# Turning the router product around in a fused conv-gate and mixture-of-experts block: router columns held, tokens streamed

## The reference, cut to what matters

```python
x = x + conv_gate(layernorm_over_channels(x))      # per sample and channel: a gate from mean, max, std and a median
t = tokens(x)                                      # 2048 tokens of 512 channels
h = layernorm(t)
logits = h @ router_w.T                            # 8 experts
top_vals, top_idx = top_k(logits, 1)
out = sigmoid(top_vals) * glu(h, expert top_idx)   # 8 experts of 512 x 512
out = out + glu(h, shared)
x = t + out
```

## Time and profile before

| what | us |
|---|---|
| median of 3 runs | 444.68 (442.83 to 445.02) |
| the profiled execution, its own time | 442.36 |
| the profiled execution, its span | 440.4 |
| TensorE matmuls busy | 402.2 |
| TensorE weight loads busy | 317.8 |
| VectorE busy | 235.2 |
| ScalarE busy | 192.8 |
| GpSimd busy | 191.8 |

### The profile page before, as it was taken

The page is one execution under the profiler, slowest core; times in us unless marked ns, Lnnn a source line. Parts: engine busy times, 40 slices in busy tenths (PEclk is TensorE's granted clock), DMA queues, the critical chain, the costliest instruction groups (busy, mean ns, idle before and its releaser), DMA issues.

```text
span 440.4 us, 7684 instructions
## 1 busy us (share of the span) xinstructions
PE 402.2 (91%) x2051; PEld 317.8 (72%) x2052; DVE 235.2 (53%) x525; ACT 192.8 (44%) x319; POOL 191.8 (44%) x262
## 2 busy tenths in 40 slices
PE   7867599899999989999999799999999999999981
PEld 3424388687878878888887687887878888777860
DVE  6879534786345442333687157456275736474330
ACT  4986257755762534542103245153264324361120
POOL 4896631555233543587021972425324340614110
PEclk9989999999999998999999899999999999999996
DMA  8900101011111551114344367626556764723100
GB/s 297 374 2 0 48 25 48 1 48 50 48 49 48 170 237 49 48 48 144 121 140 125 153 231 285 216 82 250 217 192 221 245 203 140 249 89 121 44 33 18
DMA packets 15886, 56.24 MB, mean 128 GB/s; under 512 B 2607, under 2 KB 2607, under 8 KB 12400
## 3 DMA queue, kind: packets, MB, share of 16 engines
q1 hardware_dynamic: 10976, 40.93, 25.7%
q0 software_dynamic: 4880, 14.95, 10.1%
HBM read 43.28 MB, written 13.63 MB: 129 GB/s over the span
## 4 chain that ended last, share of the span: by engine, by line
PE 75%; ACT 6%; DVE 6%; issue 5%; POOL 5%; DMA 1%; DVEq 0%; SPq 0%; POOLq 0%; ACTq 0%
PE GU L1531 42%; PE YHX L1531 22%; PE YHX L1523 3%; PE YHX L1516 3%; PE YHX L1560 2%; ACT w_raw L706 2%; ACT a_tiles L654 1%; POOL roots L434 1%; ACT hT L753 1%; ACT scratch L672 1%; PE A L1417 1%; DMA x_sb<-x_tok 1%; ACT scratch L676 1%; POOL w_parts L460 1%; POOL tok_rstd L427 1%
## 5 line engine op out<-in xcount | busy, mean ns | idle before, releaser
L1531 PE MATMUL GU<-w_parts,xT 128*128 (+1 forms) x864 | 218.4, 402 | 5.1 <-issue 4.3
L1531 PEld LDWEIGHTS GU<-w_parts,xT 128*128 128x128 f32 x864 | 159.9, 191 | 41.4 <-issue 9.9
L1531 PE MATMUL YHX<-w_parts,hT 128*128 (+1 forms) x432 | 108.2, 399 | 2.2 <-DVE hT L1099 2.2
L1531 PEld LDWEIGHTS YHX<-w_parts,hT 128*128 128x128 f32 x432 | 78.6, 188 | 19.1 <-issue 3.6
L577 POOL DMA_INDIRECT out<-x_sb,scatidx x20 | 28.8, 1438 | 105.9 <-DVE x_sb L1364 96.9
L753 ACT ACTIVATE hT<-YHX 128x512 fp32r<-128x512 f32 x36 | 21.5, 598 | 109.7 <-PE YHX L1523 109.7
L1099 DVE TENSOR_TENSOR hT<-YHX,hT 128x512 fp32r<-128x512 f32 x36 | 24.8, 690 | 71.1 <-ACT hT L753 70.9
L1105 DVE TENSOR_TENSOR hidden<-hidden,GU 128x512 f32<-128x512 f32 x36 | 24.7, 686 | 52.0 <-issue 42.7
L743 ACT ACTIVATE xT<-YHX 128x512 fp32r<-128x512 f32 x37 | 22.1, 598 | 61.8 <-PE YHX L1516 61.5
L1359 DVE TENSOR_TENSOR w_parts<-w_raw,w_parts 128x2048 f32 x19 | 43.5, 2289 | 5.0 <-ACT w_parts L852 3.2
L852 ACT ACTIVATE w_parts<-w_raw 128x2048 f32 (+1 forms) x21 | 39.4, 1912 | 0.0
(11 more groups left out here) (233 smaller groups left out, 448.8 us busy)
## 6 DMA issues: line engine op xcount, KB each, us to landing
w_raw<-weights SPq DMA_DIRECT2D x27, 1024.0 KB, 5.4
xn_d<-tiles SPq DMA_DIRECT2D x16, 256.0 KB, 2.0
z_d<-x_sb SPq DMA_DIRECT2D x16, 256.0 KB, 2.3
x_sb<-x_tok SPq DMA_DIRECT2D x7, 512.0 KB, 7.2
x_sb<-x_tok SPq DMA_DIRECT2D x2, 256.0 KB, 2.9
tiles<-xn_d,tokidx POOLq DMA_INDIRECT x21, 4.5
x_sb<-z_d,tokidx POOLq DMA_INDIRECT x20, 3.6
out<-x_sb,scatidx POOLq DMA_INDIRECT x20
```

The costliest lines, as they stand in the source:

```text
L1531: last = pe.matmul(dst, left[:, lp, kc, :], wset(q, k, wp, kc), start=(i == 0), stop=(i == 3 * KC - 1))
```

## The change

`router_parts` becomes [128, 4, 128]: 16 columns of the router as before and 112 columns of zeros, which GpSimd sets at the start (one more constant, `N_CONSTS` 18). For tiles 0 to 14 `route(t)` loads the router's 128 columns of a chunk as the stationary side and streams the two parts of the turned tile through, 256 columns in one matmul, four matmuls in all. The bank then holds, in its first 16 partitions, the logits' rows, once for each part of the tile. VectorE adds the two into `logit_rows` (16 by 128). TensorE turns these rows back (one transpose of 16 partitions, 16 columns out) at the head of `route(t + 1)`, and VectorE copies them into `logit_parts` in `keep_logits(t + 1)`. Tile 15 is routed in the old way. `logit_parts` and `logit_rows` lie in `scratch`.

```diff
-        router_parts = sb("router_parts", [P, KC, 2, E], F32R)
+        router_parts = sb("router_parts", [P, KC, P], F32R)
...
+        logit_rows = scratch[0:2 * E, 2 * C:2 * C + P]
+        logit_parts = scratch[:, 2 * C + P:2 * C + P + NT * 2 * E].rearrange("p (t e) -> p t e", e=2 * E)
...
+            pool.memset(router_parts[:, :, 2 * E:P].bitcast(F32), 0.0).then_inc(consts, 1)
...
             def keep_logits(t):
                 dve.wait_ge(logits, t + 1)
-                dve.tensor_copy(logit_parts[:, t, :], th[:, 0:2 * E]).then_inc(logits_used, 1)
+                if t:
+                    dve.tensor_copy(logit_parts[:, t - 1, :], th[:, 2 * P:2 * P + 2 * E]).then_inc(logits_used, 1)
+                if t < NT - 1:
+                    dve.tensor_reduce(logit_rows[:, :], th[0:2 * E, 0:2 * P].rearrange("p (h t) -> p t h", h=2), AX_X, ALU.add).then_inc(rows_kept, 1)
+                else:
+                    dve.tensor_copy(logit_parts[:, t, :], th[:, 0:2 * E]).then_inc(logits_used, 1)
...
                 pe.wait_ge(xlo, t + 1)
                 if t:
-                    pe.wait_ge(logits_used, t)
+                    logits_read(t - 1)
+                    pe.transpose(th[:, 2 * P:2 * P + 2 * E], logit_rows[:, :], ident[0:2 * E, 0:2 * E])
                 for kc in range(KC):
+                    if t < NT - 1:
+                        last = pe.matmul(th[:, 0:2 * P], router_parts[:, kc, :], xT[:, x_slot(t), :, kc, :],
+                                         start=(kc == 0), stop=(kc == KC - 1))
+                        continue
                     for lp in (HI, LO):
-                        last = pe.matmul(th[:, 0:2 * E], xT[:, x_slot(t), lp, kc, :], router_parts[:, kc, :, :].rearrange("p h e -> p (h e)"),
+                        last = pe.matmul(th[:, 0:2 * E], xT[:, x_slot(t), lp, kc, :], router_parts[:, kc, 0:2 * E],
                                          start=(kc == 0 and lp == HI), stop=(kc == KC - 1 and lp == LO))
                 last.then_inc(logits, 1)
+
+            def logits_read(t):
+
+                if t < NT - 1:
+                    pe.wait_ge(rows_kept, t + 1)
+                pe.wait_ge(logits_used, t if t < NT - 1 else NT)
```

More of the change, by code:

```diff
@@ L48 @@
 }
-N_CONSTS = 17
+N_CONSTS = 18
 FIRST_CONSTS = 13
@@ L156, in program @@
         warm = sb("warm", [P, 2])
-        logit_parts = sb("logit_parts", [P, NT, 2 * E])
         route_w = sb("route_w", [P, NT])
@@ L256, in program @@
         logits_used = sem("logits_used")
+        rows_kept = sem("rows_kept")
         chosen_ready = sem("chosen_ready")
@@ L1146, in _ @@
             dve.wait_ge(router_in, 16)
-            own(dve.tensor_copy(router_parts[:, :, HI, :], router_w[:, :, :]))
-            dve.tensor_tensor(router_parts[:, :, LO, :], router_w[:, :, :], router_parts[:, :, HI, :].bitcast(F32), ALU.subtract).then_inc(router_ready, 1)
+            own(dve.tensor_copy(router_parts[:, :, 0:E], router_w[:, :, :]))
+            dve.tensor_tensor(router_parts[:, :, E:2 * E], router_w[:, :, :], router_parts[:, :, 0:E].bitcast(F32), ALU.subtract).then_inc(router_ready, 1)
             measure_x1(2)
@@ L1637, in _ @@
                 visit(n, BEGIN)
-                pe.wait_ge(logits_used, max(t for m in range(n) for t in TURNED_AT.get(m, ())) + 1 if n else 2)
+                logits_read(max(t for m in range(n) for t in TURNED_AT.get(m, ())) if n else 1)
                 transpose_h(n, n % 2)
@@ L1677, in _ @@
             gate_product(n + 1, x_slot(n + 1), 0, 0)
-            pe.wait_ge(logits_used, NT - 1)
+            logits_read(NT - 2)
             transpose_h(n, 0)
@@ L1684, in _ @@
             gate_product(n + 2, x_slot(n + 2), 0, 0)
-            pe.wait_ge(logits_used, NT)
+            logits_read(NT - 1)
             transpose_h(n + 1, 1)
```

## The result

The changed kernel takes **440.23 us** (median of 7, 439.7 to 442.95) against 444.47 us before (7 runs): a ratio of 0.9924 with a 95% interval of 0.9895 to 0.9953. The forecast was 441.8 in a range of 439.2 to 445.2, with 0.57 on faster by over 0.5%. Sign, range and size came out right. The reasons did so only in part, as the two traces show.

A forecast was written before the change was run, and what follows sets the result against it. The prediction took TensorE, busy 402.2 of 440.4 us, as the bound. Nine middle tiles gave -3.0 us, tile 0 -0.14, tile 11 +0.14, tile 15 +0.11: -2.9 on 444.68, so 441.8 us, range 439.2 to 445.2.

The forecast's parts named there:

- What bounds the kernel: TensorE, 75% of the chain: shorter routes pay for twelve of sixteen tiles; at tiles 3, 4, 6, 7 TensorE only waits longer.
- Eight pairs become four of 256 columns: In each route of tiles 0 to 14, a load and matmul pair stays at 0.1125 us with 256 columns streamed.
- rival C: In each route, load and stream don't overlap at 256 columns: 0.22 us a pair, +1.8 us, 446.5; chance 0.08.
- The 98 ns a pair that the prediction set aside: Skill page's estimate for 256 columns: a middle route 0.06 us cheaper, the sum nearly 1 us better; not used.
- One transpose more: Turning the logits' rows back on TensorE costs a whole pair, 0.11 us; middle route minus 0.34 us, tile 15 plus 0.11.
- VectorE: New reduction of 256 elements at the end of `keep_logits`: 0.42 us a tile, hidden in a normal iteration.
- two places: Ahead of routes 1 and 11 TensorE waits for the reduction: 0.31 us more behind route 0, 0.48 behind route 10.
- The memset: GpSimd's zeros at the start, 448 elements a partition: at most 0.84 us, ahead of idle time, costing nothing.
- The sum: All tiles on the chain together: -2.9 us, from 444.68 to 441.8 us.
- Rival A: Behind routes 10 and 11 the clock's fall, costing 1.54 us, goes too: 440.2 us; chance 0.27.
- the prediction's remark that this fall agrees with idling: The clock's fall near 246 us, behind a wait of 2.44 us, agrees with the page tying falls to TensorE's idling.

The follow-up runs named there:

- the version with full rows: Changed kernel with the logits' rows reduced and turned back over all 128 partitions instead of 16: 439.99 us, ratio 0.9921 to the kernel before.
- the filler ahead of route 1 alone: Kernel before with two bf16 matmuls of 512 columns added between routes 0 and 1 only: 443.31 us, ratio 0.9981.
- the changed kernel without padding: Changed kernel with the router's stationary side left at 16 columns, without the zeros: 442.14 us in one execution.

## Why the prediction was right, and where it wasn't

That 440.2 us came out near the 441.8 of the forecast is in good part luck: the work on TensorE gained some 2 us less than the sum said, and the clock, which the forecast's own sum had left out, gave some 1 to 3 us.

**What bounds the kernel** held. Shorter routes come out where the chain runs through them, and for tiles 3, 6 and 7 TensorE's wait for VectorE grew by what the route lost, 0.07 us each (0.39 to 0.46 us at 88 us, for one).

**Eight pairs become four of 256 columns** at an unchanged pace: right, 0.117 us measured for 0.1125. With that rival C falls; 0.22 us a pair was nowhere seen. (The 98 ns a pair that the prediction set aside would have been worth 0.06 us on 11 tiles, some 0.65 us, not nearly 1.)

**One transpose more** is the step that failed: "It has 16 partitions but loads 128 columns, so I charge a whole pair, 0.11 us." It costs 0.35 us of idle time and then 0.16 us to the next load. With it a middle route saves 0.12 us, not 0.34, and tile 15 loses 0.34 us instead of 0.11 (its two products are 4.00 us apart for 3.66). I had looked at the load's columns only, and at rows in which every load was of 126 or 128 partitions. The Trainium skill's page "TensorE: Matmul & The Clock Gate", section "Step-by-step: what each phase is for", says that a load is pulled ahead of running matmuls when the row groups don't conflict or when it goes to the background weight buffer. That section doesn't say what becomes of a load of fewer rows behind matmuls of all rows. This case has the numbers: 0.35 us of idle time for 16 and 64 rows, none for 126 and 128.

**VectorE** was right: 0.402 us measured for 0.42, covered but for two places; the waits there are 0.73 and 0.80 us for 0.67 and 0.84 predicted. The memset took 0.48 us and is hidden.

**The sum** of 2.9 us was right for a kernel that was not the one made: the version with full rows comes to 2.84 us in the table, the changed one to 0.78. What was measured above 0.78 us I put down to the clock. It is 2.3 to 3.4 us by the medians, but 1.1 to 2.6 by the ratios, and the line through the 35 executions gives 1.5. That is worked out from whole executions; which falls each timed one had isn't known.

**Rival A** came true in that the clock is whole behind route 11, and the clock gave more than A's price. I priced one fall at 1.54 us in the profile and gave it 0.27. I did not draw the conclusion from a number that I had: the timed runs lay 2.3 us above the profiled one. Both new profiles of the kernel before have the fall near 50 us besides; so have all eight of kernels with 256-column routes, so this one is no part of the gain. That the pair of 16-column routes brings the fall at 171 us about is supported, not shown. Of four profiles with that pair as it was, two have the fall (the kernel before's three and the filler ahead of route 1 alone). Of ten with filler in it or 256-column routes, none has. But two of four is few, and filler and shorter routes also move everything behind them in time. The firmest evidence is in the timed executions: filler in both pairs makes them shorter, with an interval clear of 1.

What stays open is the fall at 246 us. A wait of 2.4 to 2.5 us stands ahead of it in the kernel before and in the changed one alike (2.44 and 2.42 us). Yet four of the fourteen profiles have the fall: two of the kernel before, the filler ahead of route 1 alone, and the changed kernel without padding. So the prediction's remark that this fall agrees with idling holds only in part: the wait alone doesn't bring it about. It may depend on when that wait falls, which no run here varied by itself. Likewise the expert part, behind the table's stretch, differs from profile to profile (177.9 to 179.6 us from the up product of its second block, behind the fall at 246 us, to the last down product) for reasons not pursued; of the changed kernel's gathers one landed so late that TensorE waited 0.91 us for it.

## What to carry to other kernels

Price a new matmul by where its load can start, not only by its columns: an operand of 16 or 64 partitions, put behind full matmuls, waited here until they had ended, and giving it all 128 partitions removed a wait of three times its own price. Stretches in which TensorE is busy by name and streams nearly nothing may cost a fall of the clock in the product behind them, so look at the granted clock after them in more than one profile. And when timed runs lie above the profiled one by about a fall's price, take another profile before forecasting.

## What I had not expected of the hardware

Loads of 16 and of 64 partitions begin 0.35 us late behind a product, about when its last matmul ends; those of 126 and 128 partitions don't. A load of 16 columns takes 94 ns where one of 128 takes 188, and does not wait. The Trainium skill's page "TensorE: Matmul & The Clock Gate", section "LDWEIGHTS (loading the stationary operand)", has the time go by columns, which for 16 would be an estimated 13 ns and for 128 an estimated 107; the rows show 94 and 188, half and not an eighth, and the measurement decides. Two matmuls of filler, 0.45 us of pointless work a pair, made a tuned kernel of 444.5 us 3.8 us faster by the medians, 2.3 by the ratio.
